# Filler matmuls between the groups of transposes that make the rows of the second attention, with the loop around them written out

## The reference

```
h = wavelet tokens of x (three Haar levels, details weighted by softmax), rows of text appended   # 8 x 288 x 256
h = h + attention0(layernorm(h))     # softmax over -0.5 * squared distance, across the 8 images
h = h + experts0(layernorm(h))       # router, top 2 of 8 experts, one shared expert
h = h + attention1(layernorm(h))     # per image: 16 heads of 16, 4 groups of keys and values, 288 positions
h = h + experts1(layernorm(h))       # router, top 2 of 8, two shared halves
```

## Time and profile before

| | before |
|---|---|
| median of 3 runs | 839.61 us (834.66 to 840.32) |
| profiled execution, its time | 839.79 us |
| its span, first to last instruction | 837.9 us |
| TensorE busy | 753.9 us (90%) |
| VectorE busy | 578.3 us (69%) |
| ScalarE busy | 340.1 us (41%) |
| granted TensorE clock, mean over the span | 0.965 |

### The profile page before, as it was taken

One profiled execution on the slowest core, in us unless ns is written; L12 is line 12 of the kernel. 1 busy time (PEld: TensorE's weight loads), 2 busy tenths in 40 slices (PEclk: granted clock), 3 DMA queues, 4 the chain that ended last, 5 costly groups with the idle time before them and its releaser, 6 DMA issues.

```text
span 837.9 us, 13657 instructions
## 1 busy us (share of the span) xinstructions
PE 753.9 (90%) x4984; PEld 611.1 (73%) x4984; DVE 578.3 (69%) x1222; ACT 340.1 (41%) x598; POOL 126.2 (15%) x121
## 2 busy tenths in 40 slices
PE   4639995799999999599999999999998999999997
PEld 4528994599999999465444444344566999999997
DVE  6295767777777777727666666466787777777776
ACT  1305444433333333213677676465415333333332
POOL 0104554000000000061112452121230000000000
PEclk9999998999999999599999999589999999999999
DMA  7210000000000000063436655300400000000000
GB/s 250 101 69 1 1 0 1 1 1 1 2 1 2 0 0 0 2 154 83 93 66 116 114 97 99 41 21 17 188 1 1 1 20 10 11 20 7 14 20 19
DMA packets 20944, 34.46 MB, mean 41 GB/s; under 512 B 6188, under 2 KB 16844, under 8 KB 20376
## 3 DMA queue, kind: packets, MB, share of 16 engines
q1 hardware_dynamic: 16136, 31.06, 14.2%
q10 hardware_dynamic: 4752, 2.66, 2.0%
HBM read 23.72 MB, written 9.95 MB: 40 GB/s over the span
## 4 chain that ended last, share of the span: by engine, by line
PE 83%; DVE 11%; ACT 2%; issue 2%; DMA 1%; SPq 0%; POOL 0%; DVEq 0%; POOLq 0%
PE PS L1212 17%; PE PS L1214 16%; PE PS L1213 16%; PE PS L1468 8%; PE PS L1443 5%; PE PS L1452 5%; PE PS L1220 3%; PE PS L1476 3%; PE PS L1557 2%; DVE MX L1124 2%; PE PS L1241 2%; PE PS L1334 1%; PE PS L1232 1%; DMA halves<-in_halves 1%; DVE xTl L924 1%
## 5 line engine op out<-in xcount | busy, mean ns | idle before, releaser
L1124 DVE TENSOR_REDUCE MX<-PS 128x2 f32<-128x576 f32 x144 | 108.9, 756 | 72.1 <-PE PS L1452 71.0
L1050 DVE SCALAR_TENSOR_TENSOR h<-PS,cmb,h 128x256 f32<-128x256 f32 (+1 forms) x342 | 143.8, 476 | 0.3 <-PE PS L1214 0.3
L666 ACT ACTIVATE PR<-PS 96x768 f32<-96x768 f32 x144 | 115.6, 806 | 62.0 <-PE PS L1443 61.1
L608 ACT ACTIVATE sg<-PS 128x384 f32<-128x384 f32 x114 | 55.9, 490 | 162.2 <-PE PS L1214 162.2
L1035 DVE TENSOR_TENSOR al<-aa,ah 128x384 fp32r<-128x384 f32 x114 | 63.6, 558 | 67.2 <-ACT ah L612 67.1
L612 ACT ACTIVATE ah<-aa 128x384 fp32r<-128x384 f32 x114 | 60.0, 526 | 84.9 <-DVE aa L1029 84.9
L1212 PE MATMUL PS<-xTh,W1h 128*128 128x384 f32 x240 | 80.6, 336 | 0.0
L1214 PE MATMUL PS<-xTl,W1h 128*128 128x384 f32 x240 | 80.4, 335 | 0.0
L1213 PE MATMUL PS<-xTh,W1l 128*128 128x384 f32 x240 | 80.4, 335 | 0.0
L1029 DVE TENSOR_TENSOR aa<-sg,PS 128x384 f32<-128x384 f32 x114 | 63.2, 554 | 24.1 <-ACT sg L608 23.5
L1212 PE MATMUL PS<-xTh,W0h 128*128 (+1 forms) x216 | 72.5, 336 | 0.0
(11 more groups left out here) (234 smaller groups left out, 1576.8 us busy)
## 6 DMA issues: line engine op xcount, KB each, us to landing
QS<-scrH SPq DMA_DIRECT2D x30, 144.0 KB, 4.4
W1raw<-in_w SPq DMA_DIRECT2D x1, 3840.0 KB, 12.7
W0raw<-in_w SPq DMA_DIRECT2D x1, 3456.0 KB, 10.8
scrH<-qh SPq DMA_DIRECT2D x8, 432.0 KB, 2.5
scrL<-ql SPq DMA_DIRECT2D x8, 432.0 KB, 3.1
out_tokens<-h SPq DMA_DIRECT2D x6, 384.0 KB, 2.3
QS<-scrL SPq DMA_DIRECT2D x15, 144.0 KB, 5.2
x_in<-in_x SPq DMA_DIRECT2D x2, 1024.0 KB, 6.3
```

The lines of the kernel that those rows point to most:

```text
L666: A_(PR[0:KT, ca:cb + 1:cb - ca, :], PS[0:KT, b:b + 2, 0:CW], ACT.Exp).then_inc(s["e_exp"], 1)
L1050: ins = V.scalar_tensor_tensor(out=hj, in0=PS[:, b + t // 2, (t % 2) * D:(t % 2) * D + D], scalar=cmb[:, ds(g * GT + t, 1), e:e + 1].squee ...
L1124: V.tensor_reduce(MX[:, hf, z:z + NSH // 2 + 1:NSH // 2], PS[:, b:b + 2, 0:POS], AX_X, ALU.max).then_inc(s["e_mx"], 1)
```

## The change

TensorE's program alone is changed. The helper `prep` loses its loop and is kept for the first experts. A new function `rows_for_images` does the six groups for the second attention, all written out. After T1, T2, T3, T4 and T5 it issues 22, 5, 5, 5 and 9 filler matmuls (`WARM_E`) of 128x128 by 384 columns, whose result in bank 4 nobody reads. Two waits are new, between T0 and T1: the last accumulation but one of the experts has left bank 4 (`f0_acc`), and `a1h` has been written, which the fillers read.

```diff
-        def prep(c, buf, off, L=None):
-            def two(r, first=False):
-                for b in range(2):
-                    g = 2 * r + b
-                    if not first:
-                        pe.wait_ge(s[f"{c}_lo"], g - 1)
-                    transpose_group(c, g, buf[:, b], 2 * b + off)
...
-            if L is None:
-                with pe.Fori(1, NG // 2) as r:
-                    two(r)
...
+        def keep_warm(n):
+
+            for _ in range(n):
+                M(PS[:, 4, 0:GW], a1h[:, 0, 0:P], a1h[:, 1, :], start=True, stop=True)
+
+        def rows_for_images():
+
+            for g in range(NG):
+                if g > 1:
+                    pe.wait_ge(s["e_lo"], g - 1)
+                transpose_group("e", g, xn1[:, g % 2], g % 2 * 2)
+                if g == 0:
+                    pe.wait_ge(s["f0_acc"], NG * 9 - 1)
+                    pe.wait_ge(s["e_a1h"], 1)
+                if g:
+                    keep_warm(WARM_E[g - 1])
...
-        prep("e", xn1, 0)
+        rows_for_images()
...
+WARM_E = [22, 5, 5, 5, 9]
```

More of the change, by code:

```diff
@@ L1351, in router_back, with prep @@
             ins.then_inc(s[f"f{L}_lgt"], 1)
-        def prep(c, buf, off, L=None):
-            def two(r, first=False):
-                for b in range(2):
-                    g = 2 * r + b
-                    if not first:
-                        pe.wait_ge(s[f"{c}_lo"], g - 1)
-                    transpose_group(c, g, buf[:, b], 2 * b + off)
[L1360 to L1364, removed]
-            if L is None:
-                with pe.Fori(1, NG // 2) as r:
-                    two(r)
[L1368 to L1374, removed]
+        def prep(c, buf, off, L):
+            for g in range(NG):
+                if g > 1:
+                    pe.wait_ge(s[f"{c}_lo"], g - 1)
+                transpose_group(c, g, buf[:, g % 2], g % 2 * 2 + off)
+                if g:
+                    router(L, c, g - 1, 6)
+                if g > 1:
+                    router_back(L, g - 2, g % 2, 7)
+            router(L, c, NG - 1, 6)
+            router_back(L, NG - 2, 0, 7)
+            router_back(L, NG - 1, 1, 7)
+        def keep_warm(n):
+            for _ in range(n):
+                M(PS[:, 4, 0:GW], a1h[:, 0, 0:P], a1h[:, 1, :], start=True, stop=True)
+        def rows_for_images():
+            for g in range(NG):
+                if g > 1:
+                    pe.wait_ge(s["e_lo"], g - 1)
[3 more added lines that the diff above has]
+                    pe.wait_ge(s["e_a1h"], 1)
+                if g:
+                    keep_warm(WARM_E[g - 1])
         def experts(L, gu):
```

## The result

The changed kernel takes 833.11 us in the median of 20 runs (829.93 to 839.01), the kernel before 837.92 us in 20 runs (832.67 to 842.47). The ratio is 0.9957, interval 0.9939 to 0.9975: 0.4% faster, clear of no change and inside my "within 1%". The ratio is the recorded one, from all runs of both, and not the quotient of the medians: the medians differ by 4.8 us, the ratio means 3.6 us with an interval of 2.1 to 5.1 us. I had counted 2.1 us. The forecast was 837.6 us, the range 829.5 to 841. Of the 4.5 us between 837.6 and 833.11, 1.9 lie in the base: I reckoned from one execution of 839.79 us, and the kernel before has a median of 837.92 us in 20 runs. The profiled execution took 833.64 us, with a span of 831.8.

A forecast was written before the change was run, and what follows sets the result against it. The prediction held TensorE, busy nine tenths of the span, slowed by lower-clock stretches. From 839.8 us, T2's delay (+1.1), faster T2 and T5 (-1.3) and image 0's projections (-1.9) gave -2.1, or 837.6 us; range 829.5 to 841.

The forecast's parts named there:

- within 1%: Whole kernel: time between 831.2 and 848.0 us, one per cent being 8.4 us; chance 0.82.
- The path: Changed stage: path crosses TensorE at T2 and T5, VectorE between; both groups at 2.4 GHz gain 1.3 us.
- the step on the clock: During the 22 fillers after T1: full clock returns at 342.0 us, so T2 starts 1.1 us late.
- The projections: Second attention's projections: at the higher clock from the start, image 0 gains 1.9 us, all 36 gain 2.5 us.
- The transfers bind: Before the first row scores: image 0's way through memory shortens 2.1 us, TensorE's 2.7; TensorE waits 0.6 us.
- the slow stretch after 500 us: Image pipeline, slices 25 and 26: goes or stays by itself, worth 7.8 us; gone gives 829.8 us, chance 0.15.
- Transposes do not lift the clock: Changed stage: only fillers raise the clock, T2 2.6 us late, 839.2 us; chance 0.18 shared with the clock falling again.
- The fillers all run at the lower clock: Gaps before T2 to T5: too many fillers at low clock, first projection 7.5 us later, up to 847.3 us; chance 0.07.
- It does nothing: Changed stage: clock falls again between T2 and T5, fillers lift nothing, 839 to 841 us; counted within a shared 0.18.

The follow-up runs named there:

- turn7: The changed kernel plus four fillers in each of three units of turn 7, where no image is projected: ratio 0.9923 to the kernel before, median 831.53 us.
- t7_no_fill: turn7 with no fillers in the changed stage (WARM_E all 0): ratio 0.9959 to the kernel before, median 834.73 us.
- t7_ahead: turn7 with 14 more fillers in the pause ahead of T0: ratio 0.9918 to the kernel before, median 830.84 us.
- no_fill: The changed kernel's written-out loop with no fillers at all: ratio 0.9997 to the kernel before, median 835.18 us.
- before_again: The kernel before, unchanged, for more runs and a second profile: ratio 0.9980 to itself, median 835.57 us.
- first_only: The changed kernel with only the 22 fillers after T1, none later: ratio 0.9985 to the kernel before, median 837.34 us.
- two_more_warm: The kernel before with 18 instead of 16 warm-up matmuls ahead of the first row scores: ratio 1.0002, median 837.11 us.
- rest_only: The changed kernel without the 22 fillers after T1, keeping the later 5, 5, 5, 9: ratio 0.9974 to the kernel before, median 834.16 us.
- t7_transposes: turn7 with the 22 fillers after T1 replaced by 26 transposes: ratio 0.9943 to the kernel before, median 832.12 us.
- after_again: The changed kernel, unchanged, for more runs and a second profile: ratio 0.9963 to the kernel before, median 832.46 us.

## Why the prediction held, and which size was off

The measured 833.11 us lies in my range, and not in the 836.8 to 838.5 us to which I had given 0.56. The mechanism in the stage held, with its gain at the lower edge of what was measured. The range reached down to 829.5 us only for the case that the later slow stretch is lost. That stretch did become rarer, in a way that my sum didn't have, so that the median lies inside the range is partly luck. The sum itself has a slip: 839.79 - 2.1 is 837.7, not 837.6.

**The path and the step on the clock.** The clock came back 5.9 us after T0 began, in the second profile 5.1 us (at 343.2) and in turn7's 3.8 us; I had taken 4.5. So T2 was late by 1.9 us (347.56 - 2.07 against 343.61), 1.5 and 0.8 us, mean 1.4, where I had 1.1. The term was small for the first profile and about right for the three, all inside its bounds of 0.2 and 3.5. The rows that I took the return from do not fix it either: in the changed kernel's profile the first experts' twelve transposes began at 140.10 at 1.2 GHz, as in the earlier trace rows, and the clock came back at 150.9 and not 3.4 us later. With 1.9 in my own sum the first projection comes at 354.1, and it did (354.10). T2 to T5 at 0.82 to 0.85 us, the fillers hidden beside VectorE, and the 9 that end just in time held.

**The projections and the transfers.** The write of image 0 was issued 1.4 us earlier than before (360.79 - 2.07 against 360.14), and the first row scores came 1.2 us earlier, behind a wait of 0.49 us for the transfers; my sum with T2 1.9 us late gives 1.3 us and a wait of 0.6. The transfers bind, as said.

**The stage in all.** Four profiles without the fillers (35.7, 36.0, 34.9, 36.1 us, mean 35.65) and three with just the change's (34.5, 33.8, 33.5, mean 33.9) give -1.7 us. The pair t7_no_fill and turn7 gives -3.2 us in the medians of 12 and 8 runs, and -2.6 us in their stages. The forecast of -2.1 lies between. What the medians have beyond the stages is not explained. The mean clock from 330 to 371 us is 0.71 to 0.75 in the first four, 0.92 to 0.96 in the three, and 1.00 in t7_ahead.

**The rest of the 4.8 us.** I had held the slow stretch after 500 us as a case by itself, "goes or stays", worth 7.8 us and unmoved by the change. That step failed in part. In all 131 runs of the kernel before, 81 lie above 836.5 us, with a median of 834.6 for the others. In 32 runs of the changed kernel 6 lie above 835.2, and the others have a median of 832.3. The lines between the heaps are drawn after the fact, and 836.5 lies in no gap. The lower heaps differ by 2.3 us, about what the stage gives, and the share in the upper heap went from six in ten to two in ten, and that moves the median further. I had given the stretch the same chance in both kernels. Its size was too large as well for most runs: the profile pair has 8.3 us, but the two heaps' medians lie 4.5 us apart in the kernel before (839.1 against 834.6) and 5.6 in the changed one. So a changed kernel without the stretch has the 832.3 us of its lower heap, and not my 829.8. That the upper heap is this stretch rests on two things. Of the profiles of kernels without turn 7's fillers, the three with a low clock for 20 us or more in turn 7 are the three executions above 839 us. And with turn 7's fillers few runs are in it: of turn7's 8 runs none, and of the 43 runs of the five kernels that have fillers in the stage as well 3 lie above 835.2 (836.1 to 837.1). t7_no_fill ends at 836.5 where no_fill went to 841.0. So it is nearly gone, not wholly.

**Why it became rarer is open.** In the three profiles with the long stretch (before, before_again, first_only) the clock falls 1.1 to 1.6 us after the transposes of turn 7 begin, at 522.7, 524.2 and 524.5 us. In those of no_fill and two_more_warm it falls 2.3 and 2.4 us after them and is back after 3.4 us. In the changed kernel's first profile it does not fall in this turn; in its second, and in rest_only's, it falls 14.1 us after them, again for 3.4 us. So a shift of a microsecond may decide, and the changed stage does shift all that follows. The runs of two_more_warm, which test that, are inconclusive, and the link is only argued. no_fill's four of twelve leave open whether the written-out loop has a part in it.

**The rivals.** "Transposes do not lift the clock" is refuted by t7_transposes, and its 839.2 us did not come. The Trainium skill, "TensorE: Matmul & The Clock Gate", Part 4, says that the full clock doesn't engage for transposes. For the fp32 transposes of this kernel the trace does not agree: 0.50 from 338.2 to 341.6 us and 1.00 after it, with nothing but transposes from 337.4 on. "The fillers all run at the lower clock" did not come either, but first_only shows its neighbour: fillers that pay the delay and lose the clock again. "It does nothing" is refuted by t7_no_fill beside turn7.

## What to carry to other kernels

If TensorE pauses for a slower engine and dense matmuls follow, fillers in the pauses can pay: here some 2 to 3 us of 835. Look first at the pause in which the clock falls; filling it kept the clock up here, though what that gains in time was not resolved. The small gaps behind must be filled too, or the clock can fall again, as in first_only. Count the fillers at the clock they will have: at half the clock a run sized for the full one takes about twice as long. And before reading a profile pair as cause and effect, look at every stretch whose clock differs: here a turn that the change doesn't touch moved more time than the stage that it does, and the spread of the runs gave a hint of it (834.66 beside 839.61 us in the first three).

## What the runs showed of the hardware that I had not expected

The same program on the same input differs by 10 us in 20 runs (832.67 to 842.47), and one of the 131 took 847.16 us. Its time at 1.2 GHz goes along: from mean clock and span the kernel before spent 43 us there in its 833.9 us run and 69 us in its 842.3 us run; the changed kernel 15 us at 829.9 and 52 us at 839.0.

A stretch with thin matmuls (on 48 to 50 rows or 32 columns of the 128 by 128 array) can stay at the lower clock although TensorE is busy: 18.58 of 20.20 us in before_again, at 0.50 throughout. In the changed kernel's first profile the same work ran at 1.00 through the whole turn. And once low it need not stay so: in after_again, no_fill, two_more_warm and rest_only it was back after 3.4 us. What decides between the two is not shown.
